# VectorE's loop in the block stage of a graph network kernel: turns of 16 chunks, with 16 places per register load

## The reference

```python
edge_index = jnp.stack([src, dst])
x = _layernorm(x + _L0_gnn_ref(x, edge_index, W1, b1, W2, b2))              # relu((x + segment_sum(x[src], dst)) @ W1 + b1) @ W2 + b2
x = _layernorm(x + _L1_gnn_ref(x, src, dst, ...))                            # two layers: relu(h @ W_self + mean of neighbours @ W_neigh + b)
x = _layernorm(x + _L2_gnn_ref(x, W, bias, edge_weight, src, dst))           # relu(segment_sum((x @ W)[src] * weight, dst) + bias)
x = _layernorm(x + _L3_gnn_ref(x, src, dst, edge_attr_20, edge_weight, edge_attr_3, ...))   # equivariant messages along the edges
```

## Time and profile before

| | |
|---|---|
| median of 3 runs | 2298.2 us (2297.6 to 2298.75) |
| profiled execution: its own time | 2299.14 us |
| profiled execution: span | 2297.3 us |
| mean granted clock of TensorE over the span | 0.914 |
| busy: TensorE | 2055.8 us (89%) |
| busy: VectorE | 1574.3 us (69%) |
| busy: GpSimd | 1251.2 us (54%) |
| busy: ScalarE | 1132.1 us (49%) |
| block stage: first addition to last addition, start to start | 391.73 to 708.03 us |

### The profile page before, as it was taken

One profiled execution on the slowest core, in us unless ns is written; L12 is line 12 of the kernel. 1 busy time (PEld: TensorE's weight loads), 2 busy tenths in 40 slices (PEclk: granted clock), 3 DMA queues, 4 the chain that ended last, 5 costly groups with the idle time before them and its releaser, 6 DMA issues.

```text
span 2297.3 us, 37124 instructions
## 1 busy us (share of the span) xinstructions
PE 2055.8 (89%) x7761; PEld 1167.5 (51%) x7761; DVE 1574.3 (69%) x4534; ACT 1132.1 (49%) x3234; POOL 1251.2 (54%) x1510
## 2 busy tenths in 40 slices
PE   4798961887888999999999799999999999999986
PEld 3454531665564555455444455555555555555545
DVE  8998752888886160110403488888888888888885
ACT  0396642777772010000010366666666666666654
POOL 1478874000004888888885356666666666666530
PEclk9598985667768999999999899999999999999998
DMA  5413020000002111121120133333333333333321
GB/s 195 155 14 88 3 69 16 0 0 0 0 0 62 39 43 21 21 62 20 20 62 14 67 98 98 100 99 101 97 97 97 99 100 101 97 97 98 98 66 45
DMA packets 75077, 146.99 MB, mean 64 GB/s; under 512 B 26829, under 2 KB 37570, under 8 KB 74631
## 3 DMA queue, kind: packets, MB, share of 16 engines
q0 software_dynamic: 44704, 95.66, 16.8%
q1 hardware_dynamic: 27356, 45.20, 5.9%
q10 hardware_dynamic: 2946, 5.28, 0.6%
HBM read 123.11 MB, written 22.40 MB: 63 GB/s over the span
## 4 chain that ended last, share of the span: by engine, by line
PE 70%; POOL 10%; DVE 10%; issue 6%; DMA 2%; DVEq 1%; ACT 1%; ACTq 0%; SPq 0%; POOLq 0%
PE ps L898 24%; PE ps L641 11%; POOL pair_table L526 10%; PE ps L660 8%; PE ps L789 5%; PE ps L836 4%; PE ps L881 3%; PE ps L883 3%; PE ps L882 3%; PE ps L884 3%; DVE adj_t L1217 1%; PE ps L788 1%; DVE dense L1406 1%; DVE dense L1405 1%; DMA pair_table<-dense 1%
## 5 line engine op out<-in xcount | busy, mean ns | idle before, releaser
L898 PE MATMUL ps<-adj_t 128*128 128x512 f32 x1288 | 615.3, 600 | 14.0 <-DVE adj_t L1643 14.0
L1109 ACT ACTIVATE adj_t<-adj_t 128x128 f32<-128x128 f32 x966 | 315.4, 389 | 211.0 <-DVE adj_t L1622 209.9
L582 POOL DMA_INDIRECT adj_t<-z_table,adj_t x322 | 309.6, 962 | 154.0 <-DVE adj_t L1632 68.4
L898 PEld LDWEIGHTS ps<-adj_t 128*128 128x128 f32 x1288 | 231.3, 189 | 249.6 <-issue 215.0
L526 POOL DMA_INDIRECT pair_table<-dense x192 | 236.6, 1232 | 130.5 <-issue 119.8
L540 POOL DMA_INDIRECT src_table<-st_two,src_rows x216 | 261.1, 1209 | 70.4 <-issue 65.2
L789 PE MATMUL ps<-dense 128*128 128x128 f32 x832 | 246.4, 416 | 0.0
L660 PE MATMUL ps<-wring,dense 128*128 128x512 f32 (+1 forms) x480 | 210.0, 600 | 4.6 <-issue 3.2
L533 POOL DMA_DIRECT2D st_two<-records x54 | 31.9, 591 | 329.1 <-DVE adj_t L1430 328.9
L788 PE MATMUL ps<-dense 128*128 128x128 bf16 x416 | 111.8, 269 | 110.7 <-ACT dense L1044 70.6
L881 PE MATMUL ps<-dense_r 128*128 128x512 f32 x322 | 200.3, 622 | 2.3 <-POOL dense_r L590 2.3
(11 more groups left out here) (274 smaller groups left out, 3786.3 us busy)
## 6 DMA issues: line engine op xcount, KB each, us to landing
src_table<-dense SPq DMA_DIRECT2D x8, 656.0 KB, 6.6
adj_t<-z_table,adj_t POOLq DMA_INDIRECT x322, 3.4
records<-dense SPq DMA_DIRECT2D x1, 5000.0 KB
adj_t<-src_table SPq DMA_DIRECT2D x73, 64.0 KB, 1.8
adj_t<-zeros SPq DMA_DIRECT2D x1, 4576.0 KB
src_table<-st_two,src_rows POOLq DMA_INDIRECT x216, 2.6
st_two<-records POOLq DMA_DIRECT2D x54, 62.5 KB, 2.1
adj_t<-zeros SPq DMA_DIRECT2D x1, 3328.0 KB, 12.1
```

The lines of the kernel that those rows point to most:

```text
L582: g.indirect_dma_start(out=zg[:, s, c, :], out_offset=None, in_=z_table, in_offset=bass.IndirectOffsetOnAxis(ap=dsti[:, s, c:c + 1].bitcas ...
L898: last = mm(bank[6 + h], oh[:, c, :], msg[:, c, h * D:(h + 1) * D], start=c == c0, stop=c == c0 + count - 1)
L1109: last = A(msg[:, c, (2 + k) * P:(3 + k) * P], msg[:, c, MSG:MSG + P], ACT.Copy, scale=side[:, s, c, C_Y - ATT + k:C_Y - ATT + k + 1])
```

## The change

VectorE's loop takes 16 chunks a turn instead of eight. One register load brings 16 places. Within a turn, the order is: wait for the block of chunk n and for the last addition, add chunk n, select chunk n + 8 into the buffer just used. So the wait for `blk_done` now stands ahead of the addition, together with that for `blk_added`, and the select has none of its own. Eight chunks are selected ahead, the first turn is written out, 24 turns run in the loop, and the last one is written out with eight selects and 16 additions. The loops of ScalarE and TensorE, the buffers and the banks stay as they are.

```diff
@@ -374,6 +374,8 @@
         SRC_STEPS = EJ // STAGED
         AB_IT = PAIR_CHUNKS // (2 * AB)
+        PLACES = 4 * AB
+        assert PAIR_CHUNKS % PLACES == 0
         L3_LOADS = 8 + 2 * PRODUCTS
@@ -1398,50 +1400,32 @@
-            def select(i, c):
-
-                n = i * (2 * AB) + c
+            def select(n, c):
                 col = n * PAIR_COLS + PAIR_AT
                 v.tensor_scalar(sel_b[:, c, 0, :], iotab[:, :], dense[:, ds(col, 1)], None, ALU.is_equal)
                 v.tensor_scalar(sel_b[:, c, 1, :], iotab[:, :], dense[:, ds(col + 1, 1)], None, ALU.is_equal).then_inc(sel_ready, 1)
 
-            block_at = []
-
-            def half(i, h, first=False, last=False):
-
-                n = i * (2 * AB) + h * AB
-                if not last:
-                    if not first:
-                        dve.wait_ge(blk_done, n - 2 * AB + 1)
-                    select(i, h * AB)
-                if not first:
-                    before = n - 2 * AB
-                    if h == 0:
-                        _, block_at[:] = nc.values_load_multi_w_load_instructions(
-                            pair_offs[0:1, ds(before, 2 * AB)], engines=[mybir.EngineType.DVE], min_val=0, max_val=AW_COLS - P,
...
-            for h in range(2):
-                half(0, h, first=True)
-            for h in range(2):
-                half(1, h)
-            with dve.Fori(2, AB_IT) as i:
-                for h in range(2):
-                    half(i, h)
-            for h in range(2):
-                half(AB_IT, h, last=True)
+            def turn(i, tail=False):
+                n0 = i * PLACES
+                _, block_at = nc.values_load_multi_w_load_instructions(
+                    pair_offs[0:1, ds(n0, PLACES)], engines=[mybir.EngineType.DVE], min_val=0, max_val=AW_COLS - P,
+                    skip_runtime_bounds_check_because="a sum of some of the steps between blocks; all of them make the last block's place")
+                for k in range(PLACES):
+                    c, n = k % (2 * AB), n0 + k
+                    dve.wait_ge(blk_done, n + 1)
+                    if not (isinstance(n, int) and n == 0):
+                        dve.wait_ge(blk_added, n)
+                    a = adj[:, :, ds(block_at[k], P)]
+                    v.tensor_tensor(a, a, bank[c][:, 0:2 * P].rearrange("p (k n) -> p k n", k=2), ALU.add).then_inc(blk_added, 1)
+                    if not tail or k < PLACES - 2 * AB:
+                        select(n + 2 * AB, c)
+
+            for c in range(2 * AB):
+                select(c, c)
+            turn(0)
+            with dve.Fori(1, PAIR_CHUNKS // PLACES - 1) as i:
+                turn(i)
+            turn(PAIR_CHUNKS // PLACES - 1, tail=True)
```

## The result

The changed kernel takes 2291.1 us (median of nine runs, 2289.7 to 2293.2); the kernel before takes 2297.4 (nine runs). The ratio is 0.9974, with a 95% interval of 0.9964 to 0.9985: 6 us faster, where 10.8 had been forecast. The profiled execution took 2292.0, with a span of 2290.2.

The account below looks back on a forecast made before the run. VectorE alone was taken to pace the block stage: turn ends 50.3, plain steps 250.9 and tail 4.3 make 305.5 us against 316.3, 10.8 less, so 2298.2 - 10.8 = 2287.4 us; range 2280 to 2296.

Parts of the forecast that it names:

- 25 turn ends and 26 loads: VectorE's loop in the block stage: 25 turn ends instead of 50, 26 loads instead of 52; turn ends 50.3 us.
- The turn end outside the load: From a turn's last addition to the next turn's first, without the load: 1.08 us, 0.77 before it and 0.31 behind.
- The load of 16 registers: VectorE's load at each turn end: 0.93 us, from 0.26 fixed and 0.042 per register; ends 0.60 and 1.19.
- A plain step stays at 0.655: Addition to addition within a turn: the engine stays the limit despite both waits ahead; 383 x 0.655 = 250.9 us.
- Select behind the addition, at nothing: Within VectorE's turn: the select following the addition costs nothing, with 2.6 us of cover for the chunk's product.
- The start: Start of the block stage: first load 0.34 longer, two selects fewer ahead of it, twice 0.16; even.
- a wait of VectorE for TensorE: Block stage: a sign that would make the prediction wrong; 25 idle pieces of "issue", each some 1.25 us, were expected.
- the longer step: Rival, plain steps: one more register operation exceeds the 0.035 us cover, step 0.71, 2308.5 us; chance 0.12.
- The doubled load: Rival, turn end: load costs per register with no fixed part, 1.19 us, 2293.9 us in all; chance 0.13.
- the flat one: Rival, turn end: the load doesn't grow with 16 registers, 0.60 us, 2279.1 us in all; chance 0.06.
- The fetch at each turn: Rival, turn ends: the longer loop leaves instruction memory, 25 x 1.8 = +45, 2332 us; chance 0.05.
- the gain lost elsewhere: Rival, block stage: another engine, TensorE the candidate, sets the pace and the stage stays at 316; chance 0.02.

Follow-up runs that it names:

- Without the loads: Changed kernel with constant places in place of the register loads, so sums go to wrong places in the matrix; 2255.4 us, one run.
- the kernel with turns of 8: Changed kernel with its new order kept, but turns of 8 chunks and loads of 8 registers; 2303.7 us, ratio 1.0026.
- the longer chain: Changed kernel with one more satisfied semaphore wait ahead of every addition; 2337.1 us, one run.
- turns of 32: Changed kernel with turns of 32 chunks and loads of 32 registers, all else the same; 2283.6 us, ratio 0.9936.
- the two probes: Changed kernel with twelve, then sixteen extra register loads of various counts on VectorE ahead of the merging of the lists; 2293.7 and 2301.6 us.
- loads of 4: Changed kernel with four loads of four registers in each turn of 16 instead of one load of 16; 2295.6 us, ratio 0.9990.

## Why the prediction was right, and where it was off

The sign and the range were right, and so was the place of the gain. The working, step by step, in us of the stage (305.5 forecast, 309.8 measured):

- *What bounds the kernel*: right. Without the loads 36 us go, and no other engine takes the pace, with TensorE at a granted clock of 1.00.
- *25 turn ends and 26 loads*: the count is right, with one detail left out. The first and the last turn have no taken branch: their ends are 1.68 and 1.76, and one other is 2.23. Together 0.8 us less than 25 equal ones.
- *The turn end outside the load*: 1.08 forecast, 2.144 - 1.102 = 1.04 measured. Its two halves: 0.77 and 0.31 forecast, 0.76 (604.54 to 605.30) and 0.29 (606.40 to 606.69) measured. 1.0 us less in all.
- *The load of 16 registers*: 0.93 forecast, 1.102 measured, 25 x 0.17 = 4.3 us more. This is the step that failed, the term "0.305 + 15 x 0.042". The two rows that it lies on were read rightly; the line through them was the mistake. They are loads of two sorts: one register left over (0.10 + 0.22) and two groups of four (0.10 + 2 x 0.25). The slope between them is that of neither. A load of 16 is 0.10 + 4 x 0.25. The fixed part is 0.10, not 0.26, so merging loads saves less than it seemed: four loads of four take 1.37 us, one of 16 takes 1.10.
- *A plain step stays at 0.655*: right for the step (0.657), and 381 of them are 1.0 us more; two odd ones of 0.98 and 0.99 add 0.7.
- *Select behind the addition, at nothing*: right within a turn, as no addition waits for a product that is late. At a turn end the order isn't free: two more instructions (L1415, L1417) stand behind the load, which the forecast had in its 0.31. What it cost beside the old order, 50 x 0.11 in the kernel with turns of 8, the prediction never set against the gain, but its sum contains it.
- *The start*: even in the forecast; the first addition came 1.2 us earlier (390.56 against 391.73), of which 0.7 lies ahead of the change (the first select at 387.95 against 388.68). *Behind the stage*: nothing, and it was 0.6.

Together: -0.8 - 1.0 + 4.3 + 1.0 + 0.7 = +4.2, which is the 4.3 that the stage lacks. Two of the five have the other sign; without this luck the forecast of the stage would have missed by 6.0.

The prediction named a wait of VectorE for TensorE as a sign against it. The profile after has 25 by name and, as the product's end at 602.2 shows, none in fact; the 25 pieces of idle time are there, of 1.4 us instead of 1.25.

Of the rivals, the longer step did not come, but its premise, a cover of 0.03, holds, and the run with the longer chain shows its price. The doubled load (1.19) and the flat one (0.60) are both wrong; the truth lies between the forecast and the doubled one, nearer to the latter. The fetch at each turn and the gain lost elsewhere did not happen, the first not even with 32 chunks a turn.

## What to carry to other kernels

Before the number of loads or branches in a loop is traded for their length, measure the load at the counts in question, in an idle stretch of the same engine; two rows of different counts are no line if the cost goes by groups of registers. Where an engine's sequencer stops at a wait that the next instruction could carry, move the wait onto the instruction first: it changes which loads are cheap. With the wait in the sequencer few long breaks are best; with the wait on the instruction many short ones are: own waits, turns of 32 and loads of four together gave 38 us here, where the changed kernel gave 6.

## What the runs showed of the hardware that I had not expected

- A register load of VectorE takes 0.10 us, 0.25 per full group of four registers and 0.22 per register left over. The first load from the table of places is 0.26 longer (1.362 against 1.102). In the two probes, which read the table before, the stage's longest is 1.116, and the first probe load is 0.23 or 0.37 above the rule. It isn't so for every table: in the earlier trace rows the longest is 0.330.
- A taken branch costs 0.08 us of the engine's time with nothing behind it, since it lies under queued selects; with a load behind it nothing covers either.
- A wait on the sequencer that is satisfied by the engine's own last instruction costs 0.20 us from the end of one addition to the next (0.62 apart at 0.42 each); carried by the addition it is 0.04 (0.46 apart).
- The same instructions at another place of the program: 0.05 or 0.15 us from a load to the next register operation, one step of a turn at 0.66 or 0.73, and perhaps 923 or 927 us for the last layer's loop. Differences of 0.1 to 0.2% between two orders of the code should be tried at more than one place before they are given a cause.
- The granted clock of TensorE in the block stage (400 to 650 us) was 0.68 before and 0.78 after, with TensorE's busy time down from 204.6 to 192.8 of 250 us. It was 0.88 with turns of 32 and 1.00 without loads, 0.60 with loads of 4 and 0.50 with the longer chain. The changed kernel gained nothing by it in this stage, as VectorE sets the pace; the next stage begins at 0.50 before and after.
